# Every second one-hot tile of the first token list made by GpSimd, eight instructions a tile

## What is computed

```python
topk_w, topk_idx = _route(x, w_router, b_router)     # 8 of 64 experts for each token
idx_flat = topk_idx.reshape(-1)
sort = jnp.argsort(idx_flat)
tok = sort // TOPK
x_sorted = x_flat[tok]                                # the rows, sorted by expert
group_sizes = jnp.bincount(idx_flat, length=e)
g = jax.lax.ragged_dot(x_sorted, we_gate, group_sizes)
u = jax.lax.ragged_dot(x_sorted, we_up, group_sizes)
o = jax.lax.ragged_dot(jax.nn.silu(g) * u, we_down, group_sizes)
y = jnp.zeros_like(x_flat).at[tok].add(o * w_sorted[:, None])
```

## Time and profile before

| what | value |
|---|---|
| time, median of 3 runs | 4442.48 us (4426.69 to 4442.54) |
| the profiled execution: its own time, its span | 4437.77 us, 4436.1 us |
| mean granted TensorE clock, as a share of full speed | 0.921 |
| busy: TensorE, VectorE, ScalarE, GpSimd | 86%, 59%, 44%, 50% |
| the stretch of the first list | 1137.1 to 1252.2 us |

### The profile page before, as it was taken

One profiled execution on the slowest core, in us unless ns is written; L12 is line 12 of the kernel. 1 busy time (PEld: TensorE's weight loads), 2 busy tenths in 40 slices (PEclk: granted clock), 3 DMA queues, 4 the chain that ended last, 5 costly groups with the idle time before them and its releaser, 6 DMA issues. The chain is left out here.

```text
span 4436.1 us, 100491 instructions
## 1 busy us (share of the span) xinstructions
PE 3828.3 (86%) x32500; PEld 3129.7 (71%) x32500; DVE 2627.8 (59%) x7922; ACT 1964.1 (44%) x4061; POOL 2233.2 (50%) x2350
## 2 busy tenths in 40 slices
PE   6999699965689999879869997999999997499991
PEld 5777577744478888757757775777777776399991
DVE  4775466658954443345546663766666665855553
ACT  2554255534223333312214443776777774155550
POOL 2333322212146666566645452777677774256665
PEclk8999799977899999989979998999999998599996
DMA  1000100000259999877740001333332331256554
GB/s 54 1 0 1 30 10 12 3 25 21 105 188 299 299 300 301 267 237 261 257 138 2 0 0 54 98 93 92 90 93 74 95 91 31 94 211 224 217 192 121
DMA packets 293459, 518.82 MB, mean 117 GB/s; under 512 B 103008, under 2 KB 136160, under 8 KB 282464
## 3 DMA queue, kind: packets, MB, share of 16 engines
q1 hardware_dynamic: 222656, 353.08, 24.1%
q0 software_dynamic: 37440, 102.29, 8.0%
q10 hardware_dynamic: 33120, 60.31, 3.6%
HBM read 375.55 MB, written 139.98 MB: 116 GB/s over the span
## 5 line engine op out<-in xcount | busy, mean ns | idle before, releaser
L2063 POOL DMA_INDIRECT L_ffn_xin<-zs,L_ffn_listed x460 | 498.5, 1084 | 298.4 <-issue 168.8
L581 POOL TENSOR_TENSOR L_xattn_p<-L_xattn_p,L_xattn_rsum 128x1024 f32<-128x1024 f32 x256 | 484.2, 1896 | 266.4 <-DVE L_xattn_rsum L685 266.4
L2426 POOL DMA_INDIRECT L_ffn_back<-ys,L_ffn_slots x320 | 314.1, 982 | 199.0 <-issue 91.5
L2095 PE MATMUL L_ffn_bank<-L_ffn_xT,L_ffn_w 128*128 128x256 f32 x1528 | 365.7, 382 | 4.5 <-ACT L_ffn_xT L2162 3.0
L714 ACT ACTIVATE L_xattn_p<-L_xattn_p,L_xattn_negmax 128x512 f32<-128x512 f32 x512 | 363.5, 716 | 2.0 <-DVE L_xattn_negmax L624 1.7
L1319 ACT ACTIVATE L_attn_pT<-L_attn_bank 128x384 f32<-128x384 f32 x512 | 223.4, 488 | 296.1 <-PE L_attn_bank L1425 157.0
L624 DVE CUSTOM_DVE_ANT_0 L_xattn_p<-L_xattn_scores,L_xattn_mask 128x512 f32<-128x512 f32 x512 | 329.6, 681 | 9.6 <-PE L_xattn_scores L784 4.1
L2162 ACT ACTIVATE L_ffn_xT<-L_ffn_bank 128x512 f32<-128x512 f32 (+1 forms) x230 | 136.7, 594 | 410.2 <-DVE L_ffn_yo L2324 199.5
L796 PE MATMUL L_xattn_turned<-ident,L_xattn_p 128*128 128x128 f32 x2048 | 282.2, 282 | 35.6 <-POOL L_xattn_p L581 20.2
L2095 PEld LDWEIGHTS L_ffn_bank<-L_ffn_xT,L_ffn_w 128*128 128x128 f32 x1528 | 277.5, 192 | 38.4 <-issue 4.8
L796 PEld LDWEIGHTS L_xattn_turned<-ident,L_xattn_p 128*128 128x128 f32 x2048 | 225.4, 142 | 98.0 <-POOL L_xattn_p L581 50.2
(11 more groups left out here) (384 smaller groups left out, 11193.5 us busy)
## 6 DMA issues: line engine op xcount, KB each, us to landing
L_ffn_w<-in_L_ffn_w SPq DMA_DIRECT2D x78, 1024.0 KB
L_ffn_w<-in_L_ffn_w SPq DMA_DIRECT2D x191, 384.0 KB
ys<-L_ffn_yo ACTq DMA_DIRECT2D x230, 256.0 KB
kv<-kv_v_row SPq DMA_DIRECT2D x128, 256.0 KB
L_xattn_k_raw<-kv SPq DMA_DIRECT2D x128, 256.0 KB, 2.7
L_xattn_v<-kv SPq DMA_DIRECT2D x16, 2048.0 KB, 9.2
kv<-kv_k_row SPq DMA_DIRECT2D x96, 256.0 KB
L_xattn_mask<-in_L_xattn_mask SPq DMA_DIRECT2D x256, 64.0 KB, 2.0
```

Source lines behind the costliest of these rows:

```text
L581: pool.tensor_tensor(p[:, s % 4, :, :], p[:, s % 4, :, :], rsum[:, s % 2, :, None].to_broadcast([P, 2, c.keys]), ALU.mult).then_inc(n_read ...
L2063: pool.indirect_dma_start(xin[j % U][:, t, :], None, zs, bass.IndirectOffsetOnAxis(ap=listed[:, 2 * j + t:2 * j + t + 1], axis=0)).then_in ...
L2095: return pe.matmul(out, a[0], b[0], start=first, stop=last)
L2426: pool.indirect_dma_start(back[:, i % NG, :], None, ys[0:NB * RB, :], bass.IndirectOffsetOnAxis(ap=slots[:, tile, k:k + 1], axis=0)).then_ ...
```

## The change

For the first list alone (`by_pool` is empty without `keys`), the tiles 5, 7, 9, ... 31 get their `hot_low` from GpSimd: eight `tensor_scalar` instructions a tile, one for each pick, each 128x128 in 16 bit, comparing with `low_f` and multiplying by 1.0. Tile t still waits until tile t-2 is consumed; the semaphore goes up after the eighth. VectorE leaves these tiles out and tells GpSimd once, before its loop, that `low_f` is ready. TensorE waits for one semaphore or the other. On GpSimd the splits of the third and fourth pair of sources now come before tiles 13 and 21.

```diff
-    def list_pool(self, pool, begun):
+    def list_pool(self, pool, begun, by_pool, one_hot):
...
         split_sources(1)
-        for j in range(2, self.QUADS):
-            split_sources(j)
+        for tile in by_pool:
+            if tile in (13, 21):
+                split_sources(2 + tile // 21)
+            one_hot(tile)
         pool.wait_ge(self.w_split, 2)
...
+        by_pool = [tile for tile in range(5, TILES, 2) if keys]
...
                 if keys:
-                    keys.list_pool(pool, owner_taken)
+                    def one_hot(tile):
+                        if tile == by_pool[0]:
+                            pool.wait_ge(parts_ready, 1)
+                        pool.wait_ge(added, (tile - 1) * K)
+                        for k in range(K):
+                            e = pool.tensor_scalar(hot_low[:, tile % 2, k, :], iota[:, 0:P], low_f[:, tile, k:k + 1], 1.0, ALU.is_equal, ALU.mult)
+                        e.then_inc(pool_low_made, 1)
+
+                    keys.list_pool(pool, owner_taken, by_pool, one_hot)
...
-                    pe.wait_ge(low_made, tile + 1)
+                    if tile in by_pool:
+                        pe.wait_ge(pool_low_made, by_pool.index(tile) + 1)
+                    else:
+                        pe.wait_ge(low_made, tile + 1 - sum(j < tile for j in by_pool))
...
+                dve.sem_inc(parts_ready, 1)
                 for i, (tile, k) in enumerate(picks):
-                    if k == 0:
+                    if k == 0 and tile not in by_pool:
```

More of the change, by code:

```diff
@@ L1923, in expert_phase @@
         low_made = sem("p_low_made")
+        pool_low_made = sem("p_pool_low_made")
+        parts_ready = sem("p_parts_ready")
+        by_pool = [tile for tile in range(5, TILES, 2) if keys]
         high_made = sem("p_high_made")
```

## The result

The changed kernel took 4487.06 us (median of 4 runs, 4484.98 to 4494.93) beside 4441.18 us for the kernel before (4 runs, 4426.69 to 4442.54): ratio 1.012, 95% interval 1.0098 to 1.0141 (the ratio comes from all runs; the two medians alone give 1.010). It is slower, by some 46 us; the forecast was 4442 with a range from 4425 to 4468. Its profiled execution took 4484.98 us beside a span of 4483.3.

What follows compares the result with a forecast made beforehand. VectorE was taken to bound the first-list stage, TensorE next. Pairs at -2.5 us and splits at +2 us summed to -0.5 us; with the runs' median of 4442.48 us this gave 4442 us, range 4425 to 4468.

Steps and rivals of the forecast that it cites:

- The bound of the kernel before: First-list stage: VectorE sets the pace at 6.92 us a pair of tiles, TensorE is next at 5.95 us.
- The price of the GpSimd instruction: GpSimd's tensor_scalar over 128x128: taken as 0.41 us start to start, from a two-input operation of the same size.
- the power row: GpSimd's slowest small instruction, the power of two elements per partition, 696 ns; taken as the upper bound of the price.
- 3.46 + 8c: VectorE's us per pair of tiles, c being the beat of one hot_high beside a burst; 6.74 us at c = 0.41.
- So it does not bind first: TensorE's side of the pair: burst 3.3, hand-overs 0.2 and tile o 2.98 us make 6.5 us, below VectorE's 6.74.
- a sign of being wrong: If TensorE waits for a GpSimd tile while VectorE is idle, the burst binds through the two buffers, not VectorE.
- The contention reading: VectorE beside a burst: one hot_high slips through per GpSimd instruction, at no cost to GpSimd; 14 pairs give back 2.5 us.
- Rival (b): Eight hot_high beside each burst: VectorE and GpSimd block each other, c 0.70 us, pair 9.06 us, time 4474; chance 0.17.
- The splits: Third and fourth source pairs' splits on GpSimd, moved between bursts before tiles 13 and 21: delay of 2 us in all.
- rival (a): GpSimd is quick: 0.31 us or less an instruction, so TensorE binds at 5.95 us a pair; time 4430, chance 0.18.
- the loss carries to the end of the kernel: Stages after the first list start when it is done, so the stage's shift, forecast as -0.5 us, carries to the end.
- the nothing for the second list: Second list: the added semaphore wait costs VectorE below 0.1 us, covered by the loop's own start.

Runs made afterwards that it cites:

- Experiment 8: The change with ScalarE making the odd tiles in GpSimd's place: 4451.36 us, ratio 1.0001, with two hot_low buffers; 4420.22 us, ratio 0.9967, with four.
- experiment 6: Kernel before plus GpSimd bursts into an unread spare tile, some bursts in other operations, sizes or data types; a single execution for its profile, 4441.33 us.
- experiment 4: The change plus 24 unused TensorE matmuls ahead of each GpSimd tile's first pick; run twice: 4483.8 us, ratio 1.011, and 4487.27 us, ratio 1.0117.
- experiment 1: Against the change: VectorE makes all 32 hot_low again, GpSimd's 14 bursts go to a spare tile nobody reads; 4449.9 us, ratio 1.0034 to the kernel before.

## Why the prediction was wrong

**The bound of the kernel before** was right: VectorE full, TensorE next (at a pair of 5.78 us rather than 5.95). Experiment 8 took the 16.0 us off VectorE, without interference, and the stage shrank by 15.1.

**The price of the GpSimd instruction** is the step that failed first. "I take 0.41 us, from the row with the same number of elements" was 0.69, close to the upper bound that I had written down from the power row and gave only to the rivals (0.70). The choice by element count was the error: in experiment 6 three operations of the same size cost 0.29, 0.37 and 0.69 us. In my own sum for VectorE, 3.46 + 8c, this price alone would have made 8.98 us a pair and lost 29 us; that is not how it was lost, since with four buffers the same instructions at the same price leave the stage at 115.8 us.

**"So it does not bind first"** is the step through which the price cost 57 us of stage. The sum of burst, hand-overs and tile o was made once, at 0.41, and came to 6.5 us against 6.74. It was not made at the upper bound. At 0.69, and with the 0.8 us by which VectorE's next hot_low holds one instruction of each burst (see below), it reads 5.5 + 0.8 + 0.2 + 2.98 = 9.5 us, and it passes 6.92 from an instruction of about 0.47 us on (0.37 if the hold is counted: with it even 0.41 gives 7.3 us). Measured at the full clock in experiment 4: 9.68 us a pair. So the margin was 0.24 us, and the price error in this sum was 8 x 0.28 = 2.2 us. I had put the loop down as a sign of being wrong (TensorE waiting for a GpSimd tile while VectorE is idle), and that sign is what the profile shows, but I gave it no price and no chance as a rival of its own.

**The clock** was missing from the sum altogether. TensorE waited 3.78 us in the pair shown (3.5 on average), its granted clock was then 0.50, and tile o, on the path, keeps GpSimd waiting 4.3 to 5.5 us for the 3.06 of experiment 4. That makes the pair 11.45 for 9.68, 13 x 1.77 = 23 us; the stages of experiment 4 say 20. By terms, then, the 57 us are some 34 of loop at full clock (149.1 - 115.1) and some 20 to 23 of clock.

**The contention reading**, one hot_high per GpSimd instruction, was wrong for this form. Around the burst shown above 12 hot_high go in 1209.22 - 1204.81 = 4.41 us, 0.37 each, and in experiment 1 eight in 1205.00 - 1202.35 = 2.65 us, 0.33 each, for 0.29 alone: two to each GpSimd instruction. They don't delay GpSimd (in the burst shown 717 to 719 ns with hot_high beside it, 713 for the last one with VectorE idle). Experiment 1 puts all of it at 12.6 us. Rival (b) came nearer, with a c of 0.70, 9.06 us a pair and a time of 4474, but by luck: its price is met, and its mechanism isn't there. hot_high and the compare did not block each other for whole instructions, and its "place" was VectorE, which is idle a third of the stage.

The Trainium skill ("SBUF — State Buffer", Who interferes with whom) says that whichever of the two engines issues first blocks the other for its whole instruction, when VectorE's is in a two-port mode, and that a two-input VectorE instruction contends with GpSimd's reads. The trace agrees for the two-input hot_low, which holds a GpSimd compare (1507 ns for 717); hot_high beside the compare shows no such block (0.33 to 0.37 us for 0.29), though it does beside the subtractions. The Trainium skill ("GPSIMD Engine Reference", Engine selection) puts one-input work at roughly line rate. The copy came at 0.29 us, the 0.30 of rival (a), and the one-input compare at 0.69, so for the compare the trace differs and rival (a) had no ground.

**The splits**, for which I set 2 us, cost nothing. They fall into GpSimd's wait for TensorE: the burst after them starts 2.14 us after they end, where the others wait 4.3 to 5.5 [the row of 1194.32 above]. **Right** were the instruction counts, that the loss carries to the end of the kernel, and the nothing for the second list (from its start to the end of the span 605.3 us before and 605.9 after).

## What to carry to other kernels

Before handing work to a slower engine, write the circle through its buffers as a sum of its own (its burst, the hand-overs, the consumer's time with that buffer) and compare it with the beat at the upper bound of every unknown price; an idle engine is no help where it may not start. Price an instruction by the same operation on that engine; where there is no such row, work the sum out with the highest row of small instructions too. Work handed over in smaller pieces, or with buffers enough for the helper to run ahead, takes the burst out of the circle, and only then does the idle time of the helper count. A wait put into the consumer's path can also lower TensorE's clock for the turn behind it, which here was some 20 of the 57 us.

## What the runs showed of the hardware

A hot_low of VectorE holds up one GpSimd instruction: the one that started at 1209.5, inside the hot_low of 1209.22 to 1210.43, took 1507 ns for 717.

```profile
L2084 POOL TENSOR_SCALAR L_ffn_hot_low<-L_ffn_iota,L_ffn_low_f x8: 713/718/1507, 1205.4 to 1211.0; 128x128 f16<-128x128 f16 x8
```

Beside the compares hot_high passes with a small loss, while beside the f32 subtractions of the splits it is still held, as in the earlier trace rows: here six took 3.33 us. GpSimd, then VectorE:

```profile
1189.66 1.26 POOL L160 TENSOR_TENSOR kv_srcT_llo<-L_ffn_yo,kv_srcT_lhi 128x512 fp32r<-128x512 f32 x1
1190.89 1.29 POOL L161 TENSOR_TENSOR kv_gridT_llo<-L_ffn_yo,kv_gridT_lhi 128x512 fp32r<-128x512 f32 x1
```

```profile
1190.12 3.33 DVE L2289 TENSOR_SCALAR L_ffn_hot_high<-L_ffn_iota,L_ffn_high_f,L_ffn_token 128x382 f16<-128x382 f16 x6 [1.01 <-PE L_ffn_bank L2158]
```

How much GpSimd disturbs VectorE thus hangs on the form of its instruction, and I can't say from these runs by what. What GpSimd's own instruction costs hangs on its operation in the same way: 0.29 us for a copy and 0.69 for a compare and multiply, both over 128x128 in 16 bit (experiment 6).

TensorE's granted clock was 0.50 after a wait of 3.8 us and stayed at 0.96 when the wait was filled with matmuls of no use. And where 336 matmuls were added in the list, a phase that begins a thousand us later took 1569.1 to 1575.6 us for 1555.2 to 1560.5, by a cause that stays open.
